# Column sums of a relation's counts: ten TensorE products over five row tiles, or VectorE's sum over the tiles and four products

## The reference, cut to what matters

```
u = x @ root + bias
for r in range(8):
    mask = (edge_type == r)
    sums = segment_sum(x[src] * mask[:, None], dst, 625)
    cnt  = segment_sum(mask, dst, 625)
    u = u + (sums / maximum(cnt, 1)[:, None]) @ weight[r]
z = concatenate([u, x]) @ w_gate + b_gate
h = tanh(u) * z + x * (1 - z)
```

## Time and profile before

| | |
|---|---|
| median of 3 runs | 1012.62 us (1012.36 to 1013.88) |
| the profiled execution, its own time | 1011.6 us |
| span of the profile, first to last instruction | 1009.8 us |
| TensorE busy (of span) | 996.9 us (99%), 5320 matmuls |
| VectorE busy | 332.9 us (33%) |
| ScalarE busy | 277.5 us (27%) |
| GpSimd busy | 253.4 us (25%) |
| DMA | 91.42 MB, mean 91 GB/s |
| granted TensorE clock, mean | 0.998 of full |

### The profile page before, as it was taken

The page is one execution under the profiler, slowest core; times in us unless marked ns, Lnnn a source line. Parts: engine busy times, 40 slices in busy tenths (PEclk is TensorE's granted clock), DMA queues, the critical chain, the costliest instruction groups (busy, mean ns, idle before and its releaser), DMA issues.

```text
span 1009.8 us, 14891 instructions
## 1 busy us (share of the span) xinstructions
PE 996.9 (99%) x5320; PEld 840.2 (83%) x5320; DVE 332.9 (33%) x722; ACT 277.5 (27%) x477; POOL 253.4 (25%) x196
## 2 busy tenths in 40 slices
PE   9999999999999999999999999999999999999997
PEld 7777678778888888888888888888988888888886
DVE  6887883631130230220220212202202203112277
ACT  4332552751121221221221222212212212122332
POOL 0000001046413223223132142241231331326730
PEclk9999999999999999999999999999999999999999
DMA  7124547056311411321321231141051041212402
GB/s 258 55 70 123 151 130 248 0 209 184 89 42 43 139 53 42 119 70 42 106 83 42 79 111 36 33 152 40 12 169 41 22 158 42 73 43 73 136 1 102
DMA packets 69005, 91.42 MB, mean 91 GB/s; under 512 B 9396, under 2 KB 35475, under 8 KB 68838
## 3 DMA queue, kind: packets, MB, share of 16 engines
q1 hardware_dynamic: 68966, 90.90, 28.7%
HBM read 75.19 MB, written 15.69 MB: 90 GB/s over the span
## 4 chain that ended last, share of the span: by engine, by line
PE 95%; DVE 2%; ACT 1%; issue 0%; POOL 0%; DVEq 0%; ACTq 0%
PE ps L1152 21%; PE ps L1154 21%; PE ps L1153 21%; PE ps L1372 9%; PE ps L1371 9%; PE ps L1232 6%; PE ps L1199 2%; PE ps L1360 1%; PE ps L1427 1%; PE ps L1426 1%; PE ps L1425 1%; PE ps L1207 1%; PE ps L1176 1%; PE ps L1209 1%; PE ps L1208 1%
## 5 line engine op out<-in xcount | busy, mean ns | idle before, releaser
L456 POOL TENSOR_TENSOR w_lo<-w_raw,w_hi 128x512 fp32r<-128x512 f32 x168 | 216.5, 1293 | 714.4 <-ACT w_hi L531 556.3
L531 ACT CAST w_hi<-w_raw 128x512 fp32r<-128x512 f32 x184 | 114.6, 623 | 459.4 <-PE ps L1154 387.1
L1152 PE MATMUL ps<-w_hi,M_hi 128*128 128x512 f32 (+1 forms) x560 | 220.8, 394 | 0.1
L1154 PE MATMUL ps<-w_lo,M_hi 128*128 128x512 f32 (+1 forms) x560 | 218.7, 391 | 0.0
L1153 PE MATMUL ps<-w_hi,M_lo 128*128 128x512 f32 (+1 forms) x560 | 218.6, 390 | 0.0
L1037 DVE SCALAR_TENSOR_TENSOR u<-ps,scale,u 128x512 f32<-128x512 f32 (+1 forms) x90 | 66.3, 744 | 416.3 <-PE ps L1154 416.3
L1371 PE MATMUL ps<-C_hi,x_hi 128*128 128x320 f32 (+3 forms) x640 | 184.4, 306 | 0.0
L1372 PE MATMUL ps<-C_hi,x_lo 128*128 128x320 f32 (+3 forms) x640 | 184.3, 306 | 0.0
L1152 PE MATMUL ps<-w_hi,M 128*128 128x512 f32 (+1 forms) x360 | 140.3, 390 | 0.0
L1154 PE MATMUL ps<-w_lo,M 128*128 128x512 f32 (+1 forms) x360 | 140.2, 390 | 0.0
L1153 PE MATMUL ps<-w_hi,M 128*128 128x512 f32 (+1 forms) x360 | 140.2, 389 | 0.0
(11 more groups left out here) (166 smaller groups left out, 739.3 us busy)
## 6 DMA issues: line engine op xcount, KB each, us to landing
w_raw<-weights SPq DMA_DIRECT2D x184, 256.0 KB, 2.9
C_dram<-Cst SPq DMA_DIRECT2D x25, 512.0 KB, 6.0
C_hi<-C_dram SPq DMA_DIRECT2D x8, 1600.0 KB, 6.9
z<-b_gate SPq DMA_DIRECT2D x5, 512.0 KB, 9.6
u<-bias SPq DMA_DIRECT2D x5, 512.0 KB, 7.9
xT_raw<-xT SPq DMA_DIRECT2D x8, 312.5 KB, 6.8
u<-x SPq DMA_DIRECT2D x4, 512.0 KB, 5.5
last_raw<-weights SPq DMA_DIRECT2D x8, 256.0 KB, 5.8
```

The source lines that it names most:

```text
L456: pool.tensor_tensor(w_lo[k % RING][:, :], w_raw[k % RING][:, :], w_hi[k % RING][:, :].bitcast(f32), ALU.subtract).then_inc(w_lo_done, 1)
L531: nc.scalar.copy(w_hi[k % RING][:, :], w_raw[k % RING][:, :]).then_inc(w_hi_done, 1)
L1152: mm(o, lhs_hi[:, k, c], w_hi[k % RING][:, :], start=opens, stop=False)
L1154: last = mm(o, lhs_hi[:, k, c], w_lo[k % RING][:, :], start=False, stop=closes_)
```

## The change

VectorE adds the five row tiles of `C_hi` into `col_sum` (128 x 640; the reduction's innermost dimension is the row tile, so it reads with a step of 640 elements), rounds it to `col_parts[:, 0]` and subtracts for the rest, `col_parts[:, 1]`. TensorE waits for this (`col_step`) and forms the edge counts with two parts by two halves, four matmuls of 320 columns. The new VectorE work (`column_sums`) stands first in half 0 of a step, ahead of `add_u` of tile 0. The edge rows lie in one buffer in `table` in place of two in `space`, and `col_sum` and `col_parts` take exactly the 7680 bytes a partition that `space` had.

```diff
-                space = sb("space", [P, NT * (D - NP)], f32, agg)
+                col_sum = sb("col_sum", [P, NP], f32, agg)
+                col_parts = sb("col_parts", [P, 2, NP], f32r, agg)
...
-        def edge_rows(b):
-            return space[0:2, b * SPLIT:(b + 1) * SPLIT]
+        edge_rows = table[0:2, :].bitcast(f32)
...
+        col_step = sem("col_step")
...
-                        sp.dma_start(edges_dram[1 - odd, :].rearrange("(b n) -> b n", b=2), edge_rows(1 - odd)).then_inc(edges_stored, 16)
+                        sp.dma_start(edges_dram[1 - odd, :].rearrange("(b n) -> b n", b=2), edge_rows).then_inc(edges_stored, 16)
...
-            def edge_counts(i, odd):
+            def column_sums(i):
+                dve.wait_ge(c_here, 16 * i + 16)
+                v.tensor_reduce(col_sum[:, :], C_hi[:, :, :].bitcast(f32).rearrange("p m n -> p n m"), X, ALU.add)\
+                 .then_inc(col_step, 1)
+                dve.wait_ge(col_step, 3 * i + 1)
+                v.tensor_copy(col_parts[:, 0, :], col_sum[:, :]).then_inc(col_step, 1)
+                dve.wait_ge(col_step, 3 * i + 2)
+                v.tensor_tensor(col_parts[:, 1, :], col_sum[:, :], col_parts[:, 0, :].bitcast(f32), ALU.subtract).then_inc(col_step, 1)
+
+            def edge_counts(i):
                 dve.wait_ge(g_ready, ITEMS * i + 1)
-                v.tensor_scalar(edge_rows(1 - odd), bank(5, 2, c=SPLIT), 1.0, None, ALU.max).then_inc(g_drained, 1)
+                v.tensor_scalar(edge_rows, bank(5, 2, c=SPLIT), 1.0, None, ALU.max).then_inc(g_drained, 1)
...
             def step_work(i, odd):
                 for half in range(2):
+                    if half == 0:
+                        column_sums(i)
                     add_u(i, odd, half, 0)
                     if half == 0:
-                        edge_counts(i, odd)
+                        edge_counts(i)
...
                     pe.wait_ge(g_drained, ITEMS * (i + 1))
-                    for m in range(NT):
+                    pe.wait_ge(col_step, 3 * i + 3)
+                    for low in range(2):
                         for b in range(2):
-                            last = mm(bank(5, 2, c=SPLIT), pick_r[:, 1 - b:3 - b], C_hi[:, m, b * SPLIT:(b + 1) * SPLIT],
-                                      start=m == 0 and b == 0, stop=m == NT - 1 and b == 1)
+                            last = mm(bank(5, 2, c=SPLIT), pick_r[:, 1 - b:3 - b], col_parts[:, low, b * SPLIT:(b + 1) * SPLIT],
+                                      start=low == 0 and b == 0, stop=low == 1 and b == 1)
                     last.then_inc(g_ready, 1)
```

## The result

The changed kernel takes **1004.99 us** (median of 4 runs, 1004.34 to 1005.44) against 1012.68 (4 runs), a ratio of 0.9926 with a 95% interval of [0.9915, 0.9938], that is 6.3 to 8.6 us less. The forecast was 1005.6 us, with a range of 1004.3 to 1009.

The account below looks back on a forecast made before the run. TensorE's gapless matmuls were taken to bound the steps. Six fewer products in each of eight steps save 7.0 us, everything added costs nothing: 1012.6 - 7.0 = 1005.6 us, range 1004.3 to 1009.

Parts of the forecast that it names:

- The six products: TensorE's edge counts: six of ten matmuls a step go, 0.146 us each, 0.876 us a step, 7.0 us in all.
- VectorE's three instructions: Reduction, copy and subtraction at the start of each step: 5.0 us together, 8.6 by the high ends, costed at nothing.
- the bound of 6.9 us: High end for VectorE's reduction, from the dearest nearby rate, 2.15 ns an element; 3.5 us was the figure taken.
- The cover: About 25.6 us of TensorE's products each step, beside which VectorE's new work was to lie for free.
- The forecast edge: VectorE's reduction could last 18.5 us, 5.8 ns an element, before TensorE stalls at the edge counts.
- The third wait: TensorE's added wait before the edge counts: 0 to 0.5 us a step, taken as 0.
- The rival that it or the turn to other weights has a price: At TensorE's edge counts: up to 0.5 us a step lost, gain falls to 3.0 us, time 1009.6 us; chance 6%.
- the rival of no effect: TensorE's ten matmuls are filler before a wait ending at a fixed time, so 1012.6 us; chance 3%.
- The rival that GpSimd is shut out: The reduction keeps GpSimd waiting, so chunk 4's `w_lo` reaches TensorE late: 1029 us, or 1018; chance 5%.
- The rival "VectorE late": VectorE's three instructions end after TensorE wants the sums at 363.8; 1051 us at 25 us of reduction; chance 1%.
- One buffer for the edge rows: One buffer was held enough, as the next write comes 78 us later; cost nothing.

Follow-up runs that it names:

- e1_ten: Changed kernel with VectorE's new work and TensorE's wait kept, but ten edge-count products on the counts again; 1012.68 us.
- e2_nosums: Changed kernel without VectorE's three instructions and TensorE's wait for them; the four products read row tiles 0 and 1 of the counts; 1005.16 us.
- e4_two: Changed kernel without the low part: the subtraction and the two products on it left out, two products stay; 1002.7 us.
- e7_reduce3: Changed kernel with VectorE's reduction done three times over; 1005.78 us (one run).
- e7_reduce4: Changed kernel with VectorE's reduction done four times over; 1055.21 us (one run).
- e3_late: Changed kernel with the column sums behind `add_u` of tile 0 instead of ahead of it; 1062.86 us (one run).
- e6_chain: Changed kernel with four additions of 640 elements, each with two SBUF inputs, in place of the reduction; 1005.45 us.

## Why the prediction was right

- **The six products are on the path, at 0.146 us each.** Shown by e1_ten (put back alone, the old time), e2_nosums (taken out alone, the new time) and e4_two (two more out, 2.3 us more). The forecast 7.0 us stands against 7.7 measured with an interval of 6.3 to 8.6, and against 8 x 0.87 = 7.0 by the distances. The distances are what bears the forecast out; that the time came within 0.6 us of it is no finer a match than the scatter of the runs.
- **VectorE's three instructions cost nothing.** Shown by e1_ten. The sum for them was wrong: 5.0 us forecast, 7.3 measured. The term that failed is the reduction, 3.5 us by a slope of rows that read neighbouring elements, 5.98 with a step of 640; it was kept within the bound of 6.9 us, and the cover made it harmless: VectorE idled for 6.3 + 9.9 = 16.1 us before `add_u`, where some 18 were forecast.
- **The cover is the products between the landing of `C_hi` and TensorE's edge counts.** Shown from both sides: e7_reduce3 just fills it, e7_reduce4 and e3_late leave it. The forecast edge, 18.5 us of reduction, was right (17.96 us fit, and 23.7 less the wait of 5.1 is 18.6).
- **The third wait costs nothing.** Shown by e1_ten, the groups at the times of before. The rival that it or the turn to other weights has a price falls with it, and the rival of no effect with the distances.
- **The rival that GpSimd is shut out.** By the prediction's own reckoning it eats a step's gain from a reduction of 4.5 us on, and at 5.99 us it would have cost 2.4 us a step. It cost nothing because its condition fails: the reduction doesn't hold GpSimd up (3.81 against 3.79 us). Here the forecast stood on the mechanism and not on its 3.5 us. Instructions that do (e6_chain) made its three subtractions 1.2 us longer together, against 3.6 us of slack ahead of the first.
- **The rival "VectorE late"** would have been mis-priced: 1051 us was reckoned for 25 us of reduction by the waits alone, and 23.7 us already give 1055.2, where the same reckoning has 1042, since each pause costs about 2 us of clock beside itself.
- **One buffer for the edge rows** was not tried by itself; e1_ten has it and loses nothing.

## What to carry to other kernels

Where one engine runs without a gap, give work to another engine if it has an idle stretch that ends later than the work would; what counts is where the instruction stands in that engine's order and not how much longer it runs. Check that place by the row of the first instruction behind it: its idle time (23.5 us here) is the cover, less the wait for the input. If the cover is missed, price the pause with the clock: beside pauses of 3.3 and of 5.1 us TensorE lost a further 1.7 to 2.8 us each time. Pauses between 0.1 and 3.3 us were not tried. And look at what a split is for: a matrix of small whole numbers has no low part, and leaving that out gave 2.3 us more.

## What the runs showed that was not expected

- A VectorE reduction that steps by 640 elements takes 1.87 ns an element in all (5990 / 3200) against 1.09 for neighbours (3486 / 3200). Where it lay mostly beside a paused TensorE it took 5.7 us and not 6.0 (all eight in e3_late 5.71, the last of four in e7_reduce4 5.68); that TensorE's reads are the reason is not shown.
- Making one instruction shorter can make the next longer: with the reduction at 3.49 us the subtraction behind it took 1.79 us in place of 0.83, as it fell into GpSimd's work.
- TensorE's granted clock, 1.00 through a 24 us run of products, was 0.50 around a pause of 3.3 us: TensorE then worked at half clock for 3.4 us in one step and 5.8 us in the next, by turns, with pauses of one length.
